# Feed-forward stages: layer-norm sums moved to ScalarE, the residual added by an identity matmul, one scale kept per FP4 block

## The chip, the cores and the metric

The kernel runs on one core of one Trainium2 chip. The metric is the device time of one execution in microseconds (us); less is better. Before the change it is 868.86 us, the median of three runs (866.7 to 873.04). A difference of about 1% is what a measurement of this kernel can tell from none.

## What is computed

The input x is 8 x 512 tokens of 128 features, all float32. Six stages follow one another, each adding to x what it computes from a layer norm of x:

```python
x = x + 0.5 * _L0_ffn_ref(_layernorm(x), router_w, w1_all, w2_all)     # mixture of 8 experts   (moe_a)
x = x + _L0_attn_ref(_layernorm(x), qkv_w, proj_w, alpha_log, beta_log) # linear attention       (linatt)
x = x + 0.5 * _L0_ffn_ref(_layernorm(x), ...)                           #                        (moe_b)
x = x + 0.5 * _L1_ffn_ref(_layernorm(x), w_gate, w_up, w_down)          # FP4 feed-forward       (ffn_a)
x = x + _L1_attn_ref(_layernorm(x), ...)                                # softmax over the batch (att)
x = x + 0.5 * _L1_ffn_ref(_layernorm(x), w_gate, w_up, w_down)          #                        (ffn_b)
```

The change touches the two FP4 feed-forward stages:

```python
def fp4_quant_dequant(x):                       # blocks of 16 along the last axis
    scale = jnp.maximum(jnp.max(jnp.abs(xb), axis=-1, keepdims=True) / 6.0, 1e-12)
    idx = jnp.searchsorted(_MID, jnp.abs(xb / scale))
    return _GRID[idx] * jnp.sign(xb / scale) * scale
def fp4_linear(x, w):
    return jnp.einsum('bsk,nk->bsn', fp4_quant_dequant(x), fp4_quant_dequant(w))
h = jax.nn.silu(fp4_linear(x, w_gate)) * fp4_linear(x, w_up)    # 128 -> 352 features
return fp4_linear(h, w_down)                                    # 352 -> 128
```

## The kernel before

x stays in SBUF from the first stage to the last (`x_sb`, 32 tiles of 128 tokens x 128 features). Each engine runs its own program, written by hand in order, and semaphores join them; no scheduler moves anything. A feed-forward stage takes x in 8 groups (`GROUPS`) of 4 tiles (`TPB`), 512 tokens a group. Its engines run a body of one group each, and the bodies of different engines work on different groups at the same time:

- **VectorE (DVE), `ffn` at L1052**: body(i) first takes the layer-norm statistics of group i+2 (`ln_stats`: four BN_STATS at L754, four BN_AGGR at L761), then multiplies silu(gate) by up for group i (L1085), quantises that product to FP4 (h4), and between h4's divide and its snap adds the down product of group i-1 to x (`residual`, L1059) and starts the quantisation of the normalised x of group i+2 (x4). The class `Fp4` has the steps: `largest` (L700), `scales` (two small instructions, L706 and L708: a negated scale for the end and a nudged one for the reciprocal), `inverse` (L713), `divide` (L717), `snap` (L723), `unbias` (L728), `rescale` (L734). `snap` waits for a magnitude that ScalarE makes of the divided values (L406).
- **ScalarE (ACT), `ffn` at L611**: body(i) normalises group i+2 (`normal`, L435, four tiles), makes the magnitude of group i's h (L406, 1408 elements a row), applies silu and copies up for group i+1 (L625, L627), with the magnitude of x of group i+2 among them, copies the transposed x of group i+2 out of PSUM (`evac_xnT`, L442) and the four transposed tiles of hq of group i (`hidden_T`, L631).
- **TensorE (PE), `ffn` at L1456**: body(i) runs the gate and up products of group i+1, the transposes of x of group i+2 (L1483), the transposes of the quantised h of group i (L1470), and its down products (`down`, three matmuls a tile into PSUM bank 7, L1171 as all products).
- **GpSimd (POOL), `ln_group`**: from mean and variance the two columns with which ScalarE normalises.
- **SyncE** writes each group of the result to DRAM when the residual of the last stage is in (`x_done`).

The order inside ScalarE's body matters here:

```python
if ahead:
    act.wait_ge(s["tr_done"], i + 2)
    normal(i + 2)
act.wait_ge(s["h_divided"], i + 1)
magnitude(fq_h[0], fq_h[1]).then_inc(s["h_sized"], 1)
```

Between four `hidden_T` of group i-1 and the magnitude of group i there is only `normal`. All engines' queues are strictly in order, so whatever is put there is in front of the magnitude.

Of the kernel before, what the change touches and what calls it, by code (L numbers as in the profile page):

```python
# [38 lines left out]
ATT_EPS = 1e-6  # L39
MAGIC = 1.5 * 2.0 ** 22  # L40
TIE = 2.0 ** 100

# [32 lines left out]
def macaron(nc, x, qkv_w, proj_w, alpha_log, beta_log, router_w, w1, w2,  # L75
            in_w, in_b, out_w, out_b, w_gate, w_up, w_down, out):
    with ExitStack() as ctx:
# [36 lines left out]
        negmean = sb("negmean", [P, 8])  # L114
        shift = sb("shift", [P, 8])
        xn = sb("xn", [P, 8, C])
        xnT = sb("xnT", [P, 8 * P])
# [60 lines left out]
        def bank(k, *dims):  # L178
# [7 lines left out]
            if len(dims) == 3:  # L186
# [10 lines left out]

        s_passed_dve, s_passed_pe, s_passed_pool = sem("s_passed_dve"), sem("s_passed_pe"), sem("s_passed_pool")
        PHASES = ["moe_a", "linatt", "moe_b", "ffn_a", "att", "ffn_b"]
        NAMES = ["dve_chain", "pool_chain", "var_ready", "rstd_ready", "xn_ready",  # L200
# [11 lines left out]
                    "h_divided", "h_sized", "x_divided", "x_sized", "hq_ready",  # L212
                    "htr_done", "hT_ready", "down_done"],
        }
# [7 lines left out]
        def group_b(i):  # L222
            return x_sb[:, ds(i * TPB, TPB), :]
# [57 lines left out]
        def _(pool):  # L281
# [22 lines left out]


            ln_group(S["moe_a"], 0, TPB)

# [38 lines left out]
            for ph in PHASES:  # L346
# [18 lines left out]
                elif ph == "att":  # L365
# [13 lines left out]
                    add_bias(TPB - 2)  # L379
                    add_bias(TPB - 1)  # L380
                else:
                    with pool.Fori(1 if ph in ("moe_a", "moe_b") else 0, GROUPS) as i:
                        ln_group(s, i, TPB)
# [3 lines left out]
        def _(act):  # L387
# [31 lines left out]
            def fp4_weights_out():  # L419

                act.wait_ge(s_prep_pe, 4)
                nc.scalar.activation(gateT[:, :], bank(3, FK), ACT.Copy).then_inc(s_prep_act, 1)
                act.wait_ge(s_prep_pe, 5)
                nc.scalar.activation(upT[:, :], bank(4, FK), ACT.Copy).then_inc(s_prep_act, 1)
                act.wait_ge(s_prep_pe, 6)
                nc.scalar.activation(downT[:, :, :], bank(5, 3, P), ACT.Copy).then_inc(s_prep_act, 1)
# [184 lines left out]
            def ffn(s, first):  # L611
# [44 lines left out]
                x_magnitude(0)  # L656
                evac_xnT(s, 0)
# [3 lines left out]
                evac_xnT(s, 1)  # L661
                with act.Fori(0, GROUPS - 2) as i:
                    body(i, True, False)
                body(GROUPS - 2, False, False)
                body(GROUPS - 1, False, True)

            moe(S["moe_a"], S["linatt"], True)
# [9 lines left out]
        def _(dve):  # L677
# [5 lines left out]
            class Fp4:  # L683
# [19 lines left out]
                def scales(self):  # L703
# [3 lines left out]

                    self.t = self.ch.add(nc.vector.tensor_scalar(self.rs, self.mx, (1.0 + 2.0 ** -22) / 6.0, 1e-12,  # L708
                                                                 ALU.mult, ALU.max))

                def inverse(self):
                    self.ch.need(self.t)
                    self.t = self.ch.add(nc.vector.reciprocal(self.rs, self.rs))  # L713

# [337 lines left out]
            def ffn(s, first):  # L1052
                ch = Chain(dve, s["dve_chain"])
                hflat = hid[:, :, :].rearrange("p j f -> p (j f)")

                def residual(i):

                    dve.wait_ge(s["down_done"], i * TPB + TPB)
                    nc.vector.scalar_tensor_tensor(group_b(i), bank(7, TPB, C), 0.5, group_b(i),  # L1059
                                                   ALU.mult, ALU.add).then_inc(s["x_done"], 1)  # L1060

                def x_stream(i):
# [5 lines left out]
                def x_alone(i):  # L1068
                    dve.wait_ge(s["xn_ready"], i + 1)
                    x4 = x_stream(i)  # L1070
                    x4.largest()
                    x4.scales()
                    x4.inverse()
                    x4.divide()
# [3 lines left out]

                def body(i, ahead, behind):

                    if ahead:
                        ln_stats(s, ch, i + 2, TPB, tile_b)

# [7 lines left out]
                    h4.largest()  # L1091
                    h4.scales()
                    h4.inverse()
                    h4.divide()
                    if behind:
                        residual(i - 1)
                    if ahead:
                        dve.wait_ge(s["xn_ready"], i + 3)
                        x4 = x_stream(i + 2)
                        x4.largest()  # L1100
                        x4.scales()
                        x4.inverse()
                        x4.divide()
# [14 lines left out]
                pre = ch.k  # L1118
                ch.start(pre)
                body(0, True, False)  # L1120
                pre += ch.k
                with dve.Fori(1, GROUPS - 2) as i:
                    ch.start((i - 1) * PER["ffn"] + pre)
                    body(i, True, True)
                    assert ch.k == PER["ffn"], ("ffn", ch.k)
                pre += (GROUPS - 3) * PER["ffn"]
                ch.start(pre)
                body(GROUPS - 2, False, True)
                body(GROUPS - 1, False, True)
# [4 lines left out]
                residual(GROUPS - 1)  # L1134
                dve.wait_ge(s["x_done"], GROUPS)
# [10 lines left out]
        def _(pe):  # L1146
# [309 lines left out]
            def ffn(s, first):  # L1456
# [11 lines left out]
                def hidden_transposes(i, j):  # L1468
                    for k in range(3):
                        t = nc.tensor.transpose(bank(5 + j % 2, 3, P)[:, k, :], hq[:, j, P * k:P * k + P], ident[:, :])  # L1470
                    t.then_inc(s["htr_done"], 1)

                def down(i, j):
                    pe.wait_ge(s["hT_ready"], i * TPB + j + 1)
                    for k in range(3):
                        t = mm(bank(7, TPB, C)[:, j, :], hqT[:, j % 2, k, :], downT[:, k, :], start=k == 0, stop=k == 2)
                    t.then_inc(s["down_done"], 1)
# [23 lines left out]
                x_transposes(1)  # L1501
                with pe.Fori(0, GROUPS - 2) as i:
                    body(i, True, False)
# [12 lines left out]

PER = {"moe": 21, "linatt": 8, "att": 24, "ffn": 20}

# [21 lines left out]
```

## Time and profile before

| | |
|---|---|
| median of three runs | 868.86 us |
| the profiled execution, its own time | 870.8 us |
| its span | 869.0 us (1.8 us lie around it) |
| mean granted TensorE clock | 0.896 of full |
| busy: PE, DVE, ACT, POOL | 703.0, 676.8, 466.8, 164.6 us |
| moe_a / linatt / moe_b | about 0 to 143 / 143 to 282 / 282 to 413 us |
| ffn_a / att / ffn_b | about 413 to 562 / 562 to 712 / 712 to 867 us |

"PE busy" counts matmuls that overlap each other; the granted clock has two levels, 1.0 (2.4 GHz) and 0.5 (1.2 GHz), and what lies between in a table is a mean over a stretch. In the timeline rows below a start-to-start distance is the time that an instruction takes of its engine; the duration beside it is up to 0.1 us longer, since neighbours overlap. A float32 product counts as two matmul records, a transpose as one.

### The profile page before, as it was taken

Reading aid. Unit: us, or ns where it says so; the run is one execution under the profiler, and the core shown is the slowest. Engines: PE = TensorE matmul, PEld = TensorE weight load, DVE = VectorE, ACT = ScalarE, POOL = GpSimd, SP = SyncE. Lnnn points to the kernel's source line nnn. Section 1 sums busy time; section 2 is a strip of 40 time slices with the busy share of each in tenths; the row PEclk is TensorE's granted clock in tenths of the full one; section 3 lists DMA queues with packets and bytes.
Section 4 is the critical chain, followed back from the end, with each engine's and each line's share of the span. In section 5 each row is a group of like instructions: output and inputs, shape, how many; then the busy total and the mean of one; then the engine's idle time right before and its main releaser. Section 6 shows DMA issues by size and latency. Waiting matters only on the chain.

```text
span 869.0 us, 17382 instructions
## 1 busy us (share of the span) xinstructions
PE 703.0 (81%) x6018; PEld 533.8 (61%) x6018; DVE 676.8 (78%) x1671; ACT 466.8 (54%) x893; POOL 164.6 (19%) x323
## 2 busy tenths in 40 slices
PE   3999999798986999999585777468989865857774
PEld 2777776677775677776354665436686663546654
DVE  2888787375656578789799999649899956999995
ACT  3787777656460677777464455264323114644552
POOL 4001021645542100101111210022110001112100
PEclk9999999899999899999768788868999987687888
DMA  7000000000000000000000000000000000000000
GB/s 197 2 0 0 0 1 2 3 3 2 0 3 3 1 1 0 0 1 0 1 0 0 0 0 0 1 0 1 1 0 0 1 0 1 12 12 12 12 24 25
DMA packets 13454, 6.99 MB, mean 8 GB/s; under 512 B 1177, under 2 KB 13409, under 8 KB 13409
## 3 DMA queue, kind: packets, MB, share of 16 engines
q1 hardware_dynamic: 10464, 5.26, 2.3%
q10 hardware_dynamic: 2944, 1.12, 0.5%
q8 instruction: 29, 0.48, 0.2%
q14 instruction: 17, 0.13, 0.0%
HBM read 4.28 MB, written 2.10 MB: 7 GB/s over the span
## 4 chain that ended last, share of the span: by engine, by line
PE 60%; DVE 26%; issue 7%; ACT 3%; DMA 1%; POOL 1%; DVEq 0%; SPq 0%; POOLq 0%; ACTq 0%
PE ps L1171 53%; PE ps L1470 4%; DVE ffn_work L723 3%; DVE shared L998 2%; DVE ffn_work L728 2%; DVE picked L900 2%; PE ps L1483 2%; DVE hq L734 1%; DVE x_sb L819 1%; DVE xn L734 1%; ACT xn L435 1%; DVE ffn_work L717 1%; DVE fq_x_max L700 1%; DMA wraw<-ttn_out_proj_weight_dram 1%; DVE attT L906 1%
## 5 line engine op out<-in xcount | busy, mean ns | idle before, releaser
L1171 PEld LDWEIGHTS ps<-w_sb,sq_h 128*128 128x128 f32 x1024 | 131.9, 192 | 68.8 <-ACT sq_h L457 50.7
L819 DVE SCALAR_TENSOR_TENSOR x_sb<-ps,gates,x_sb 128x128 f32 (+1 forms) x512 | 147.8, 345 | 20.4 <-PE ps L1171 12.3
L294 POOL TENSOR_SCALAR vareps<-meanvar 128x4 f32<-128x4 f32 (+1 forms) x44 | 25.0, 568 | 606.4 <-DVEq L763 606.4
L1171 PE MATMUL ps<-w_sb,sq_h 128*128 128x128 f32 x1024 | 138.0, 278 | 0.9 <-ACT sq_h L457 0.9
L1171 PE MATMUL ps<-xnT,w_sb 128*128 128x512 f32 x256 | 135.4, 613 | 0.0
L453 ACT ACTIVATE relu_h<-ps 128x512 f32<-128x512 f32 x128 | 75.7, 591 | 57.6 <-PE ps L1171 57.3
L435 ACT ACTIVATE xn<-x_sb,shift,rstd 128x128 f32 (+1 forms) x192 | 79.8, 481 | 18.3 <-POOL shift L302 18.2
L457 ACT ACTIVATE sq_h<-relu_h 128x512 f32<-128x512 f32 x128 | 80.6, 630 | 4.0
L1483 PE MATMUL ps<-ident,xn 128*128 128x128 f32 x64 | 16.8, 414 | 70.8 <-DVE xn L734 70.8
L1171 PE MATMUL ps<-ident,shared 128*128 128x128 f32 x512 | 64.6, 290 | 10.3 <-DVE shared L998 10.3
L1171 PE MATMUL ps<-downT,hqT 128*128 128x128 f32 x384 | 71.2, 339 | 0.5 <-ACT hqT L631 0.5
L1171 PEld LDWEIGHTS ps<-ident,shared 128*128 128x128 f32 x512 | 63.0, 205 | 13.6 <-DVE shared L998 12.7
L1171 PEld LDWEIGHTS ps<-downT,hqT 128*128 128x128 f32 x384 | 63.6, 246 | 7.4 <-ACT hqT L631 5.8
L1171 PE MATMUL ps<-gateT,xnT 128*128 128x352 f32 x128 | 55.3, 516 | 12.0 <-ACT ffn_work L625 9.2
L631 ACT ACTIVATE hqT<-ps 128x384 f32<-128x384 f32 x64 | 31.2, 491 | 56.6 <-PE ps L1470 54.0
L442 ACT ACTIVATE xnT<-ps 128x512 f32<-128x512 f32 x40 | 23.9, 597 | 69.5 <-PE ps L1483 64.7
L1483 PEld LDWEIGHTS ps<-ident,xn 128*128 128x128 f32 x64 | 11.0, 207 | 79.4 <-DVE xn L734 71.1
L1470 PE MATMUL ps<-ident,hq 128*128 128x128 f32 x192 | 43.8, 373 | 16.7 <-DVE hq L734 16.7
L342 POOL TENSOR_TENSOR shared<-shared 128x128 f32<-128x128 f32 x112 | 51.0, 455 | 28.5 <-ACT shared L508 20.3
L1171 PE MATMUL ps<-upT,xnT 128*128 128x352 f32 x128 | 53.3, 500 | 0.0
L754 DVE BATCH_NORM_STATS2 stats<-x_sb 128x6 f32 (+1 forms) x192 | 41.2, 279 | 13.3 <-DMA x_sb<-in_L_attn_x_dram 9.9
L406 ACT ACTIVATE ffn_work<-ffn_work 128x512 f32<-128x512 f32 (+2 forms) x33 | 33.1, 1003 | 30.2 <-DVE ffn_work L717 30.2
(147 smaller groups left out, 1270.1 us busy)
## 6 DMA issues: line engine op xcount, KB each, us to landing
x_sb<-in_L_attn_x_dram SPq DMA_DIRECT2D x8, 256.0 KB, 6.4
out_dram<-x_sb SPq DMA_DIRECT2D x8, 256.0 KB, 2.3
w_sb<-in_L_ffn_w_all_dram ACTq DMA_DIRECT2D x2, 512.0 KB, 7.4
wraw<-in_L_attn_qkv_w_dram SPq DMA_DIRECT2D x1, 192.0 KB
wraw<-attn_in_proj_weight_dram SPq DMA_DIRECT2D x1, 192.0 KB
fraw<-in_L_ffn_w_down_dram SPq DMA_DIRECT2D x1, 176.0 KB, 3.5
fraw<-in_L_ffn_w_gate_dram SPq DMA_DIRECT2D x1, 128.0 KB, 4.0
fraw<-in_L_ffn_w_up_dram SPq DMA_DIRECT2D x1, 128.0 KB, 3.1
```

The costliest lines, as they stand in the source:

```text
L342: nc.gpsimd.tensor_tensor(st[:, k, :], st[:, k, :], st[:, k - 1, :], ALU.add).then_inc(s["prefix_ready"], 1)
L406: return nc.scalar.activation(m, v, ACT.Abs, scale=2.0 ** 22)
L435: a = nc.scalar.activation(xn[:, into + j, :], tile(i, j), ACT.Identity, scale=rstd[:, j:j + 1], bias=shift[:, j:j + 1])
L453: nc.scalar.activation(relu_h[:, e % 2, :], bank(2 + e % 2, T), ACT.Relu).then_inc(s["relu_done"], 1)
L457: nc.scalar.activation(sq_h[:, e % 2, :], relu_h[:, e % 2, :], ACT.Square).then_inc(s["sq_ready"], 1)
L631: nc.scalar.activation(hqT[:, j % 2, :, :], bank(5 + j % 2, 3, P), ACT.Copy).then_inc(s["hT_ready"], 1)
L723: self.t = self.ch.add(nc.vector.scalar_tensor_tensor(self.v, self.m, MAGIC, self.v, ALU.max, ALU.add))
L754: ch.add(nc.vector.bn_stats(stats[:, j, :], tile(i, j)))
L819: t = nc.vector.scalar_tensor_tensor(tile_b(i, j), bank(4 + e % 4, TPB, C)[:, j, :], gates[:, j, e:e + 1], tile_b(i, j), ALU.mult, ALU.add)
L1171: return nc.tensor.matmul(o, a, b, start=start, stop=stop, **kw)
L1470: t = nc.tensor.transpose(bank(5 + j % 2, 3, P)[:, k, :], hq[:, j, P * k:P * k + P], ident[:, :])
L1483: t = nc.tensor.transpose(bank(0, TPB, P)[:, j, :], xn[:, start + j, :], ident[:, :])
```

## The change

In both feed-forward stages:

1. The layer-norm statistics of groups 2 to 7 go from VectorE to ScalarE. `ln_sum` (four ACTIVATE Copy with `accum_out`) sums each token's features; GpSimd makes the negated mean; `ln_squares` (four ACTIVATE Square with that bias and `accum_out`) sums the squares; GpSimd makes the rest (`ln_from_sums`). Their full output goes to a tile `spare` that nobody reads.
2. The residual add leaves VectorE. `x_under` on TensorE puts x into PSUM bank 7 by one product with the identity, the down products accumulate on it, and `x_out` on ScalarE copies the sum back to x. The factor 0.5 is now in the down weights.
3. `scales` becomes `nudged_scales`, one small instruction less a quantisation; the sign and the nudge go into the weights.

```diff
@@ ScalarE
+                def x_out(i):
+                    act.wait_ge(s["down_done"], i * TPB + TPB)
+                    act.sem_inc(s_passed_act, 1)
+                    nc.scalar.activation(group_b(i), bank(7, TPB, C), ACT.Copy).then_inc(s["x_done"], 1)
+
+                def ln_sum(i):
+                    for j in range(TPB):
+                        a = nc.scalar.activation(spare[:, j, :], tile_b(i, j), ACT.Copy, accum_out=sums[:, 0, j:j + 1])
+                    a.then_inc(s["sum_ready"], 1)
+
+                def ln_squares(i):
+                    act.wait_ge(s["mean_ready"], i - 1)
+                    act.sem_inc(s_passed_act, 1)
+                    for j in range(TPB):
+                        a = nc.scalar.activation(spare[:, j, :], tile_b(i, j), ACT.Square, bias=negmean[:, j:j + 1],
+                                                 accum_out=sums[:, 1, j:j + 1])
+                    a.then_inc(s["square_ready"], 1)
+
-                def body(i, ahead, last):
+                def body(i, ahead, last, further=False):
                     if ahead:
 
                         act.wait_ge(s["tr_done"], i + 2)
                         normal(i + 2)
+                    if not (type(i) is int and i == 0):
+                        x_out(i - 1)
+                    if further:
+                        ln_sum(i + 3)
                     act.wait_ge(s["h_divided"], i + 1)
                     magnitude(fq_h[0], fq_h[1]).then_inc(s["h_sized"], 1)
...
+                    if further:
+                        ln_squares(i + 3)
                     if ahead:
                         evac_xnT(s, i + 2)
...
                 normal(1)
+                ln_sum(2)
+                ln_squares(2)
                 x_magnitude(0)
@@ VectorE
-                def residual(i):
-
-                    dve.wait_ge(s["down_done"], i * TPB + TPB)
-                    nc.vector.scalar_tensor_tensor(group_b(i), bank(7, TPB, C), 0.5, group_b(i),
-                                                   ALU.mult, ALU.add).then_inc(s["x_done"], 1)
...
-                    if ahead:
-                        ln_stats(s, ch, i + 2, TPB, tile_b)
...
-                    h4.scales()
-                    h4.inverse()
+                    h4.nudged_scales()
+                    h4.inverse(h4.sl)
                     h4.divide()
-                    if behind:
-                        residual(i - 1)
@@ TensorE
+                def x_under(i):
+
+                    if not (type(i) is int and i == 0):
+                        pe.wait_ge(s["x_done"], i)
+                    mm(bank(7, TPB, C), ident[:, :], group_b(i), start=True, stop=False, skip_group_check=True)
...
                         x_transposes(i + 2)
+                    x_under(i)
                     pe.wait_ge(s["hq_ready"], i + 1)
                     hidden_transposes(i, 0)
```

How the programs stand, first ScalarE, in the loop of ffn_a, from the last tile of `normal` to the magnitude. `xn` is the normalised x, `ffn_work` with 1408 columns the magnitude, with 352 columns silu. Before:

```order
L435 ACTIVATE xn<-x_sb,shift,rstd 128x128
L638 REGISTER_ALU
L406 ACTIVATE ffn_work<-ffn_work 128x1408
L624 ISA
L625 ACTIVATE ffn_work<-ps 128x352
```

The same place after the change, where the lines have other numbers (of the four sums the first and the last are shown):

```order
L461 ACTIVATE xn<-x_sb,shift,rstd 128x128
L660 ISA
L662 ISA
L662 ACTIVATE x_sb<-ps 128x512
L666 ISA
L666 ACTIVATE spare,sums<-x_sb 128x128
...
L666 ACTIVATE spare,sums<-x_sb 128x128
L686 REGISTER_ALU
L432 ACTIVATE ffn_work<-ffn_work 128x1408
```

A copy of 512 columns, behind a wait for the down products, and four ACTIVATEs with an accumulator now stand between `normal` and the magnitude.

TensorE, in the same loop, from the transposes of x to the first down products (`ps<-ident,xn` are the transposes of x, `ps<-ident,hq` those of h). Before:

```order
L1480 REGISTER_ALU
L1483 MATMUL ps<-ident,xn 128x128 x4
L1470 MATMUL ps<-ident,hq 128x128 x6
L1474 ISA
L1171 MATMUL ps<-downT,hqT 128x128 x3
```

and after the change:

```order
L1533 REGISTER_ALU
L1536 MATMUL ps<-ident,xn 128x128 x4
L1217 ISA
L1217 MATMUL ps<-x_sb,ident 128x512
L1516 MATMUL ps<-ident,hq 128x128 x6
L1526 REGISTER_ALU
L1217 MATMUL ps<-downT,hqT 128x128 x3
```

One product of 512 columns now stands between the transposes of x, which come last from VectorE, and those of h.

## Rows read from the trace of the kernel before

**Rows 1.** Timeline of DVE: start us, us, operation, in brackets idle before.
```profile
495.43 0.86 DVE L754 BATCH_NORM_STATS2 stats<-x_sb 128x6 f32 x4
...
497.06 1.63 DVE L1085 TENSOR_TENSOR ffn_work<-ffn_work 128x1408 f32<-128x1408 f32 x1 [0.23 <-DVE meanvar L761]
...
500.37 0.21 DVE L706 TENSOR_SCALAR fq_h_s<-fq_h_max 128x88 f32<-128x88 f32 x1
...
503.27 0.69 DVE L1059 SCALAR_TENSOR_TENSOR x_sb<-ps,x_sb 128x512 f32 x1 [0.18 <-PE ps L1171]
503.87 0.68 DVE L700 TENSOR_REDUCE fq_x_max<-xn 128x32 f32<-128x512 f32 x1
...
505.88 1.62 DVE L723 SCALAR_TENSOR_TENSOR ffn_work<-ffn_work 128x1408 f32<-128x1408 f32 x1
...
511.93 0.69 DVE L734 TENSOR_TENSOR xn<-ffn_work,fq_x_s 128x512 f32<-128x512 f32 x1
...
514.17 1.63 DVE L1085 TENSOR_TENSOR ffn_work<-ffn_work 128x1408 f32<-128x1408 f32 x1 [0.24 <-DVE meanvar L761]
...
529.64 1.62 DVE L1085 TENSOR_TENSOR ffn_work<-ffn_work 128x1408 f32<-128x1408 f32 x1
...
542.79 1.62 DVE L1085 TENSOR_TENSOR ffn_work<-ffn_work 128x1408 f32<-128x1408 f32 x1
```

**Rows 2.** Timeline of ACT in the same round of ffn_a.
```profile
502.12 1.65 ACT L435 ACTIVATE xn<-x_sb,shift,rstd 128x128 f32 x4
503.67 1.36 ACT L406 ACTIVATE ffn_work<-ffn_work 128x1408 f32<-128x1408 f32 x1
```

**Rows 3.** Timeline of PE in the same round.
```profile
495.56 1.11 PE L1483 MATMUL ps<-ident,xn 128*128 128x128 f32 x4 [4.61 <-DVE xn L734]
496.47 1.49 PE L1470 MATMUL ps<-ident,hq 128*128 128x128 f32 x6
497.90 1.65 PE L1171 MATMUL ps<-downT,hqT 128*128 128x128 f32 x6
499.34 0.85 PE L1470 MATMUL ps<-ident,hq 128*128 128x128 f32 x3
...
501.10 0.49 PE L1470 MATMUL ps<-ident,hq 128*128 128x128 f32 x3
...
502.94 0.76 PE L1171 MATMUL ps<-gateT,xnT 128*128 128x352 f32 x2
```

**Rows 4.** Busy us (instructions) by stretch: PE, PEld, DVE, ACT, POOL; then PEclk, DMA, GB/s.
```profile
494.00:495.00 1.00, 0.00 (x0) 0.00 (x0) 0.96 (x3) 0.00 (x0) 0.00 (x0) 0.55 0.00 0
500.00:501.00 1.00, 1.00 (x7) 1.00 (x7) 0.93 (x4) 0.49 (x1) 0.40 (x2) 0.54 0.00 0
...
607.00:608.00 1.00, 1.00 (x7) 1.00 (x6) 1.00 (x2) 0.00 (x0) 0.00 (x0) 0.50 0.00 0
```

**Rows 5.** Timeline of PE in att, just ahead of the last stretch of rows 4.
```profile
605.69 9.04 PE L1171 MATMUL ps<-ident,shared 128*128 128x128 f32 x64 [2.27 <-DVE shared L998]
```

**Rows 6.** Timeline of PE in moe_b, a product of 512 columns and its neighbour.
```profile
289.47 1.02 PE L1171 MATMUL ps<-xnT,w_sb 128*128 128x512 f32 x2
290.33 1.05 PE L1171 MATMUL ps<-w_sb,sq_h 128*128 128x128 f32 x8
```

**Rows 7.** Groups by line and shape: xcount | busy us, mean ns of one | idle before.
```profile
L435 ACT ACTIVATE xn<-x_sb,shift,rstd 128x128 f32 x128 | 53.4, 481 | 0.0
...
L417 ACT ACTIVATE wT<-ps 128x128 f32<-128x128 f32 x1 | 0.3, 273 | 0.0
```

**Rows 8.** Timeline of PE, then of ACT, in the last but one group of ffn_a.
```profile
542.92 0.87 PE L1470 MATMUL ps<-ident,hq 128*128 128x128 f32 x6 [0.90 <-DVE hq L734]
...
546.35 0.49 ACT L631 ACTIVATE hqT<-ps 128x384 f32<-128x384 f32 x1 [0.51 <-PE ps L1470]
```

**Rows 9.** Timeline of ACT at the start of ffn_a and of ffn_b: the first magnitude of x.
```profile
416.21 0.63 ACT L406 ACTIVATE ffn_work<-ffn_work 128x512 f32<-128x512 f32 x1 [0.88 <-DVE ffn_work L717]
...
720.12 0.61 ACT L406 ACTIVATE ffn_work<-ffn_work 128x512 f32<-128x512 f32 x1
```

More of the change, by code:

```diff
@@ L40 @@
 MAGIC = 1.5 * 2.0 ** 22
+NUDGE = 2.0 ** -22
 TIE = 2.0 ** 100
@@ L115, in macaron @@
         shift = sb("shift", [P, 8])
+        sums = sb("sums", [P, 2, TPB])
+        spare = sb("spare", [P, TPB, C])
         xn = sb("xn", [P, 8, C])
@@ L301, in ln_group, with ln_from_sums @@
                 pool.wait_ge(s["pool_chain"], 3 * i + 3)
+                nc.gpsimd.tensor_tensor(shift[:, 0:n], negmean[:, 0:n], rstd[:, 0:n],
+                                        ALU.mult).then_inc(s["rstd_ready"], 1)
+            def ln_from_sums(s, i, n):
+                pool.wait_ge(s["sum_ready"], i - 1)
+                pool.sem_inc(s_passed_pool, 1)
+                nc.gpsimd.tensor_scalar(negmean[:, 0:n], sums[:, 0, 0:n], -1.0 / C, None,
+                                        ALU.mult).then_inc(s["mean_ready"], 1)
+                pool.wait_ge(s["square_ready"], i - 1)
+                pool.sem_inc(s_passed_pool, 1)
+                nc.gpsimd.tensor_scalar(vareps[:, 0:n], sums[:, 1, 0:n], 1.0 / C, LN_EPS, ALU.mult,
+                                        ALU.add).then_inc(s["moment_chain"], 1)
+                pool.wait_ge(s["moment_chain"], 2 * (i - 2) + 1)
+                nc.gpsimd.tensor_tensor(rstd[:, 0:n], vareps[:, 0:n], minus_half[:, 0:n],
+                                        ALU.pow).then_inc(s["moment_chain"], 1)
+                pool.wait_ge(s["moment_chain"], 2 * (i - 2) + 2)
                 nc.gpsimd.tensor_tensor(shift[:, 0:n], negmean[:, 0:n], rstd[:, 0:n],
@@ L380, in _ @@
                     add_bias(TPB - 1)
+                elif ph in ("ffn_a", "ffn_b"):
+                    ln_group(s, 0, TPB)
+                    ln_group(s, 1, TPB)
+                    with pool.Fori(2, GROUPS) as i:
+                        ln_from_sums(s, i, TPB)
                 else:
-                    with pool.Fori(1 if ph in ("moe_a", "moe_b") else 0, GROUPS) as i:
+                    with pool.Fori(1, GROUPS) as i:
                         ln_group(s, i, TPB)
@@ L661, in ffn @@
                 evac_xnT(s, 1)
-                with act.Fori(0, GROUPS - 2) as i:
-                    body(i, True, False)
+                body(0, True, False, True)
+                with act.Fori(1, GROUPS - 3) as i:
+                    body(i, True, False, True)
+                body(GROUPS - 3, True, False)
                 body(GROUPS - 2, False, False)
                 body(GROUPS - 1, False, True)
+                x_out(GROUPS - 1)
             moe(S["moe_a"], S["linatt"], True)
@@ L1071, in x_alone @@
                     x4.largest()
-                    x4.scales()
-                    x4.inverse()
+                    x4.nudged_scales()
+                    x4.inverse(x4.sl)
                     x4.divide()
@@ L1077, in x_alone, with body @@
                     x4.rescale()
-                def body(i, ahead, behind):
-                    if ahead:
-                        ln_stats(s, ch, i + 2, TPB, tile_b)
+                def body(i, ahead, further):
                     dve.wait_ge(s["up_ready"], i * TPB + TPB)
@@ L1118, in ffn @@
                 pre = ch.k
[L1119 to L1123, printed above, removed]
+                with dve.Fori(0, GROUPS - 3) as i:
+                    ch.start(i * PER["ffn"] + pre)
                     body(i, True, True)
                     assert ch.k == PER["ffn"], ("ffn", ch.k)
[L1126 to L1129, printed above, removed]
+                ch.start((GROUPS - 3) * PER["ffn"] + pre)
+                body(GROUPS - 3, True, False)
+                body(GROUPS - 2, False, False)
+                body(GROUPS - 1, False, False)
                 if first:
@@ L1475, in down @@
                     for k in range(3):
-                        t = mm(bank(7, TPB, C)[:, j, :], hqT[:, j % 2, k, :], downT[:, k, :], start=k == 0, stop=k == 2)
+                        t = mm(bank(7, TPB, C)[:, j, :], hqT[:, j % 2, k, :], downT[:, k, :], start=False, stop=k == 2,
+                               skip_group_check=True)
                     t.then_inc(s["down_done"], 1)
@@ L1501, in ffn @@
                 x_transposes(1)
-                with pe.Fori(0, GROUPS - 2) as i:
+                body(0, True, False)
+                with pe.Fori(1, GROUPS - 2) as i:
                     body(i, True, False)
@@ L1513, in _ @@
             ffn(S["ffn_b"], False)
-PER = {"moe": 21, "linatt": 8, "att": 24, "ffn": 20}
+PER = {"moe": 21, "linatt": 8, "att": 24, "ffn": 10}
 _INS = ['L0_attn_x', 'L0_attn_qkv_w', 'L0_attn_proj_w', 'L0_attn_alpha_log', 'L0_attn_beta_log',
```

24 lines of the change are left out of this document (14 added, 10 removed).

## The prediction

> **What bounds the kernel now.** I read the whole-span table first, then the chain that ended last, then, since the change touches only ffn_a and ffn_b, the timelines of DVE, ACT and PE over one round of ffn_a. A round runs from one L1085 of VectorE to the next: 497.06 to 514.17, 17.11 us, and four rounds of a stage are alike [rows 1]. In it VectorE has hardly an idle moment: 0.23 us ahead of L1085 and 0.18 ahead of L1059 [rows 1]. PE stands idle for 4.61 us and waits for VectorE's last instruction, the rescaled x [rows 3]. So VectorE's own work sets the round.
>
> There is a second limit close behind, a ring through three engines. I count it from the start of the transposes of x on PE, at 495.56 [rows 3]:
> - transposes of x and h and the down products interleaved with their copies: ACT has made its last hqT copy at 502.12, so 6.56 us [rows 2, 3];
> - `normal` of the next group, to 503.67: 1.55 [rows 2];
> - the magnitude of h, 1.36: done at 505.03 [rows 2];
> - VectorE from the snap of h (505.88) to the end of x's rescale (511.93 + 0.69 = 512.62): 6.74 [rows 1]; hand-overs, 0.07 together.
>
> That is 16.28 us. The magnitude was ready 0.85 us before VectorE took it up; the ring has 0.83 us to spare in a round of 17.11. It has no more than that, and all the work that the change adds to ACT and PE must be looked for in it.
>
> The clock belongs to this ring. It falls to half (1.2 GHz) while PE waits (0.55 on the mean in the microsecond from 494) and is full again only at about 500.9 (0.54 in the microsecond from 500) [rows 4]; so the transposes and the first down products of every round run at half clock.
>
> **The change part by part.**
>
> VectorE loses the statistics, 495.43 to 497.06, 1.63 us; L1059 with its idle, 0.18 + (503.87 - 503.27) = 0.78; and one small scale in each of two quantisations (the longer 0.21 us, and overlapped with its neighbours, so I take 0.2 for both) [rows 1]. Its own work falls from 17.11 to 14.5 us a round. If VectorE stayed the bound, this would be the round.
>
> But the ring grows by three terms, all of which stand in its order as the programs show:
>
> *x_under on PE*, between the transposes of x and those of h. One product of 512 columns takes 0.86 us at full clock, from 289.47 to 290.33 [rows 6]. At half clock it is twice that, 1.72, as six transposes take 1.43 (496.47 to 497.90) there [rows 3]. I lay it into the round of rows 3: transposes of h start at 2.63 instead of 0.91 after the start, first down product at 4.06, end at 5.50. By then the clock is up (it rose 5.4 us after the start [rows 4]), and the second down product, 1.12 us at mostly half clock before (start at 499.34 + 0.64, to 501.10), takes 0.76 and the transposes beside it 0.33 instead of 0.64. The last hqT copy ends about 1.05 us later than before, at 7.61. If the clock rises no earlier, all 1.72 count.
>
> *x_out on ACT*: 512 columns out of PSUM, 0.5 us after `normal` (a copy of 384 columns takes 0.49 [rows 8]). Its wait for the down products costs nothing, since they end under `normal` (502.94, before 503.67 [rows 2, 3]).
>
> *ln_sum on ACT*: no row shows an ACTIVATE with an accumulator. Below, a plain one of 128 columns takes 273 ns, 0.18 us apart when it overlaps its neighbour as the others do; above, the one with two pointer operands takes 481 ns, 0.39 apart (1.55 for four) [rows 2, 7]. The accumulator's result has to be written too, which might cost still more than a pointer; I set twice the upper row, 0.8, as the far end. For the sum, without pointers, I take the middle of the two rows, 0.29, four are 1.16; for the squares, with one pointer, 0.39, four are 1.56. The Trainium skill, "ScalarE: Activation LUTs", section "What ACT_TABLE_LOAD costs", gives 186 ns + 0.833 ns a column, 93 ns more for each pointer operand and 93 ns overlap between neighbours. The trace agrees for L435 (479 by the page, 481 measured). By it, an accumulator being free, the four sums would be 0.8 us instead of 1.16 and each round 0.36 shorter; it gives no price of the accumulator.
>
> The ring is then 7.61 + 1.55 + 0.50 + 1.16 + 1.36 + 6.74 + 0.07 = 19.0 us, against VectorE's 14.5. VectorE waits about 4.5 us a round, at the snap of h, for the magnitude. The bound moves from VectorE to the ring, and the round gets longer: 19.0 against 17.11.
>
> *ln_squares* stand behind the silus and cost nothing in the rounds: the magnitude ends at 12.2 after the start of the ring, silus and the magnitude of x take about 3.7, the squares 1.56, together 17.4 of 19.0. They have 1.6 us of cover; at 0.8 us apiece they would take it all.
>
> Now one stage, from the first L1085 on.
> - First body: only VectorE's saving counts, since its magnitude isn't late: -1.85.
> - Four full rounds, 514.17 being the end of the last: 4 x (19.0 - 17.11) = +7.6.
> - The body from 514.17 to 529.64, 15.47 [rows 1]: `normal` and x_out, no ln_sum: 19.0 - 1.16 = 17.8: +2.4.
> - The body to 542.79, 13.15 [rows 1]: x_out after the down products (8.5), 0.5, magnitude 1.36, then snap to the end of h, 4.86 as before: 15.3: +2.1.
> - Last body: nothing; the copy by ACT takes the place of L1059's 0.69.
> Together +10.2 for each of the two stages.
>
> *The start of each stage.* ln_sum(2), the mean on GpSimd and ln_squares(2) stand in front of the first magnitude of x, for which VectorE waits. In ffn_a ACT was idle for 0.88 us ahead of it [rows 9]; 1.16 + 0.4 (mean and hand-overs) + 1.56 = 3.1 less 0.88: +2.2. In ffn_b it had no idle [rows 9]: +3.1.
>
> Sum, with the clock at half at the start of each round: 2 x 10.2 + 5.3 = +25.7.
>
> **The clock.** In warm rounds the ring is shorter. The last but one group shows it: from the transposes of h at 542.92 to the last copy's end at 546.84, 3.92 [rows 8]. With 0.45 and 0.86 in front: 5.23 instead of 7.61, so a ring of 16.6. PE's idle before x's transposes would be about 3.8 us instead of 4.61 (gate and up products j = 2, 3 wait for silu, which comes after the magnitude). Is that enough for the clock to fall? In att it fell after only 2.27 us of idle [rows 4, 5]. So most rounds will be cold; I take one in four to be warm, three of 12 over both stages, 3 x 2.4 = -7.2. That leaves +18.5 on the profiled execution's 870.8. The median of the runs, 868.86, is 0.2% below it; on that basis I forecast 887.
>
> **The rivals.**
> - *The clock stays up* (chance 0.20). Rounds of 16.6: per stage -1.85 - 4 x 0.5 - 0.2 for the two shorter bodies = -4.1; with the starts -8.2 + 5.3 = -2.9: 866 us, no difference that can be measured. For it: PE is busy at either side of a shorter idle. Against it: the fall after 2.27 us.
> - *The change does what it says* (0.10): VectorE remains the bound at 14.5, because ACT reaches the magnitude in time. Per stage -1.85 - 4 x 2.6 - 1.0 (15.47 to 14.5) = -13.3, with the starts -26.6 + 5.3 = -21: 848 us. This is the side of faster. It decides at a ring of under 17.1: it would need a copy done and sums finished before the down products' end, that is ACT's magnitude no later than 505.9 in the row's time; against it stands the strict order of ACT's program. A weaker form, warm rounds with sums 0.18 apart, gives 16.2 a round and about 860.
> - *The accumulator is dear* (0.08): at 0.8 apiece the sums cost 2.0 us more in each of eight full rounds and each start 3.7 more: +24 on 887, 911. At 0.5 apiece, 0.84 a round and 1.3 a start: +9, 896.
> - The forecast, cold rounds for the most part: 0.62, own range 876 to 897.
>
> **The numbers.** Slower by over 1% (above 877.5) holds nearly all of the forecast and the dear accumulator, 0.69; within 1% the rest of it and the warm rival, 0.21; faster 0.10. The range goes from a little under the warm rival, 864, to a little over the forecast with the accumulator at 0.5, 899.
>
> **What would show it.** VectorE idle for 2 us or more ahead of the snap of h in each full round, released by ACT's magnitude (right), or none (the second rival). Rounds between L1085s of 19.0 cold and 16.6 warm. On ACT `normal`, x_out, four sums and the magnitude without a gap; the sums' spacing, 0.29 or not. x_under at 1.7 us and a PEclk of 0.5 from before x's transposes. The first snap of x in ffn_b 3.1 us later after `normal`. Wrong would be: PE out of the chain that ended last in the two stages, or PEclk at 1.0 through them.

## The result, and the profile after

| | before | after |
|---|---|---|
| median of the runs | 869.64 us (866.7 to 873.04) | 886.79 us (886.09 to 889.69) |
| the profiled execution, its span | 870.8, 869.0 us | 889.69, 888.0 us |
| busy: PE, DVE, ACT | 703.0, 676.8, 466.8 us | 708.9, 649.5, 505.7 us |

The change makes the kernel slower: 1.0206 times the time of before, 95% interval 1.0168 to 1.0244. In the two profiled executions VectorE is busy 27 us less and the kernel takes 19 us longer: taking work off VectorE brought no time.

In the waits of DVE in the kernel after (us in total, times, longest), two lines lead into the feed-forward:

```profile
DVE fq_x_max L755 <- ACT xn L461: 29.6, 10, 3.7
DVE ffn_work L784 <- ACT ffn_work L432: 27.8, 16, 5.6
```

The first is the first step of x's quantisation, which waits for `normal`; the second is the snap of h, which waits for the magnitude. DVE's timeline of one cold round of ffn_a (cold: PE's clock is at half through its first part), to hold against [rows 1] (L1137 is L1085 of before, L784 is L723):

```profile
503.93 1.62 DVE L1137 TENSOR_TENSOR ffn_work<-ffn_work 128x1408 f32<-128x1408 f32 x1
...
508.21 1.62 DVE L778 TENSOR_TENSOR ffn_work<-ffn_work,fq_h_r 128x1408 f32<-128x1408 f32 x1
513.57 0.69 DVE L755 TENSOR_REDUCE fq_x_max<-xn 128x32 f32<-128x512 f32 x1 [3.73 <-ACT xn L461]
...
516.48 1.62 DVE L784 SCALAR_TENSOR_TENSOR ffn_work<-ffn_work 128x1408 f32<-128x1408 f32 x1 [0.90 <-ACT ffn_work L432]
...
523.15 1.62 DVE L1137 TENSOR_TENSOR ffn_work<-ffn_work 128x1408 f32<-128x1408 f32 x1
```

19.22 us from L1137 to L1137, where it was 17.11 [rows 1]; 3.73 + 0.90 = 4.63 of them idle. ACT in this round, to hold against [rows 2] (L657 copies hqT, L461 is `normal`, L662 x_out, L666 the sums, L432 the magnitude):

```profile
511.33 0.49 ACT L657 ACTIVATE hqT<-ps 128x384 f32<-128x384 f32 x1 [0.51 <-PE ps L1516]
511.89 1.65 ACT L461 ACTIVATE xn<-x_sb,shift,rstd 128x128 f32 x4
513.44 0.57 ACT L662 ACTIVATE x_sb<-ps 128x512 f32 x1
513.92 0.30 ACT L666 ACTIVATE spare<-x_sb 128x128 f32 x1
514.12 0.19 ACT L666 ACTIVATION_READ_ACCUMULATOR spare<-x_sb 128x1 f32 x1
514.21 0.30 ACT L666 ACTIVATE spare<-x_sb 128x128 f32 x1
...
515.09 1.36 ACT L432 ACTIVATE ffn_work<-ffn_work 128x1408 f32<-128x1408 f32 x1
```

and PE, against [rows 3] (the second line is x_under):

```profile
504.07 1.11 PE L1536 MATMUL ps<-ident,xn 128*128 128x128 f32 x4 [3.80 <-DVE xn L795]
504.97 1.92 PE L1217 MATMUL ps<-x_sb,ident 128*128 x2
506.68 1.49 PE L1516 MATMUL ps<-ident,hq 128*128 128x128 f32 x6
508.11 1.65 PE L1217 MATMUL ps<-downT,hqT 128*128 128x128 f32 x6
```

The ring can be read off step by step: transposes of x at 504.07 to the last hqT copy's end at 511.82, 7.75; `normal` 1.55 and 0.07 of hand-over; x_out 0.48; four sums 1.17; the magnitude 1.36; snap (516.48) to the end of x's rescale, 6.75; with the small hand-overs 19.2.

Not all rounds are alike. The L1137s of ffn_a are 14.42, 18.05, 19.07, 18.13, 19.22, 16.83 and 14.53 us apart, those of ffn_b within 0.13 of these. The second to the fifth are the full rounds, those with `ln_sum`. Each has a stretch at half clock. In the two longer ones it ended 5.7 and 6.0 us after the start of x's transposes, in the two shorter ones 3.2 and 3.7 us after it. In three of the four it began ahead of the transposes; in the fourth, whose transposes began at 485.94, the clock fell 0.23 us behind their start, and they took less than the 1.11 us of the cold round:

```profile
485.94 0.94 PE L1536 MATMUL ps<-ident,xn 128*128 128x128 f32 x4 [3.81 <-DVE xn L795]
```

Two stretches of the granted clock (the column behind POOL) show the difference, for this short round and for the long one above:

```profile
489.00:490.00 1.00, 0.99 (x6) 0.66 (x5) 0.93 (x3) 0.67 (x2) 0.00 (x0) 0.71 0.00 0
...
509.00:510.00 1.00, 1.00 (x7) 1.00 (x7) 0.84 (x1) 0.00 (x0) 0.00 (x0) 0.50 0.00 0
```

Where the 19.0 us of span are, from the same events in both traces: start of ffn_a (from `normal(1)` to the first L1085 or L1137) +2.7, its bodies +6.7, start of ffn_b +3.5, its bodies +6.5. That is 19.4; the stages that the change does not touch differ by +2.7 (before ffn_a) and -3.0 (att), which I take for the difference between two executions: over the 14 traces of this document, which share their code there, the start of `normal(1)` in ffn_a lies between 412.93 and 416.77, and the time from the last write of x in ffn_a to the start of `normal(1)` in ffn_b between 152.8 and 156.3 us.

The added time does not come from a colder clock. From the first to the eighth L1085 or L1137 of ffn_a the mean granted clock is 0.79 before and 0.87 after, and in ffn_b the same: PE is at half clock for less time than before, and the rounds are longer all the same.

### The profile page after: what moved, and what is told of

It is laid out like the page before. It is cut to its first block, busy times and chain, and to the rows that moved or that the text cites. A ratio compares the mean times of both kernels' runs of the same rounds, so it can differ in the third digit from the quotient of the medians.

```text
span 888.0 us, 17404 instructions
## 1 busy us (share of the span) xinstructions
PE 708.9 (80%) x6050; PEld 526.4 (59%) x6050; DVE 649.5 (73%) x1527; ACT 505.7 (57%) x1101; POOL 165.8 (19%) x323
## 4 chain that ended last, share of the span: by engine, by line
PE 58%; DVE 23%; ACT 8%; issue 7%; POOL 1%; DMA 1%; ACTq 1%; SPq 0%; DVEq 0%; POOLq 0%
PE ps L1217 51%; DVE ffn_work L784 3%; PE ps L1516 3%; DVE ffn_work L789 2%; DVE shared L1059 2%; ACT xn L461 2%; ACT ffn_work L432 2%; DVE picked L961 2%; PE ps L1536 2%; ACT spare L666 1%; DVE hq L795 1%; DVE xn L795 1%; DVE x_sb L880 1%; DVE attT L967 1%; DMA wraw<-ttn_out_proj_weight_dram 1%
## 5 line engine op out<-in xcount | busy, mean ns | idle before, releaser
L298 POOL TENSOR_SCALAR vareps<-meanvar 128x4 f32<-128x4 f32 (+1 forms) x32 | 7.7, 240 | 442.6 <-DVEq L824 442.6
L461 ACT ACTIVATE xn<-x_sb,shift,rstd 128x128 f32 (+1 forms) x192 | 79.7, 480 | 17.0 <-POOL shift L306 16.5
L1536 PE MATMUL ps<-ident,xn 128*128 128x128 f32 x64 | 15.0, 379 | 70.3 <-DVE xn L795 70.3
L1217 PEld LDWEIGHTS ps<-ident,shared 128*128 128x128 f32 x512 | 61.2, 200 | 15.2 <-DVE shared L1059 14.7
L657 ACT ACTIVATE hqT<-ps 128x384 f32<-128x384 f32 x64 | 30.9, 490 | 65.6 <-PE ps L1516 64.1
L1217 PE MATMUL ps<-downT,hqT 128*128 128x128 f32 x384 | 60.8, 303 | 1.1 <-ACT hqT L657 1.0
L784 DVE SCALAR_TENSOR_TENSOR ffn_work<-ffn_work 128x512 f32<-128x512 f32 (+2 forms) x33 | 38.3, 1161 | 27.8 <-ACT ffn_work L432 27.8
L1217 PEld LDWEIGHTS ps<-downT,hqT 128*128 128x128 f32 x384 | 53.1, 210 | 7.7 <-ACT hqT L657 6.1
L1217 PEld LDWEIGHTS ps<-gateT,xnT 128*128 128x128 f32 x128 | 24.5, 211 | 43.6 <-ACT ffn_work L651 30.7
L1516 PEld LDWEIGHTS ps<-ident,hq 128*128 128x128 f32 x192 | 31.8, 184 | 30.1 <-DVE hq L795 16.4
```

The lines of the kernel that those rows point to most:

```text
L461: a = nc.scalar.activation(xn[:, into + j, :], tile(i, j), ACT.Identity, scale=rstd[:, j:j + 1], bias=shift[:, j:j + 1])
L657: nc.scalar.activation(hqT[:, j % 2, :, :], bank(5 + j % 2, 3, P), ACT.Copy).then_inc(s["hT_ready"], 1)
L784: self.t = self.ch.add(nc.vector.scalar_tensor_tensor(self.v, self.m, MAGIC, self.v, ALU.max, ALU.add))
L1217: return nc.tensor.matmul(o, a, b, start=start, stop=stop, **kw)
L1536: t = nc.tensor.transpose(bank(0, TPB, P)[:, j, :], xn[:, start + j, :], ident[:, :])
```

## The experiments

All are the kernel after the change ("after") with the edit shown, unless it says otherwise. What a run gained is its median against the 886.79 us of after; ratios are to the kernel before, whose median on these chips was 869.96 to 870.96 us, up to 1.3 us above the 869.64 of the result, so a gain may be larger by up to that. Round times are the distances of L1137 (or the line that answers to it) in ffn_a, without the last body.

**sums_later.** The four sums leave the ring.

```diff
-                    if further:
-                        ln_sum(i + 3)
                     act.wait_ge(s["h_divided"], i + 1)
...
                     if further:
+                        ln_sum(i + 3)
                         ln_squares(i + 3)
```

> Based on the changed kernel (886.8 us); the four sums of the group ahead stand behind the silus instead of between normal and the magnitude of h. Theory (a ring through PE, ACT and VectorE sets the round, and these 1.16 us are a term of it): each of 8 full rounds gets shorter by about 1.16 us, from 18.6 to 17.5, and the time falls to about 877.5. Rival (ScalarE is simply loaded, it doesn't matter where the sums stand): no change, 885 to 888.

878.46 us, 1.0079 (1.0053 to 1.0106): 8.3 us gained. Rounds 14.42, 17.07, 17.26, 17.32, 17.18, 16.94, 14.72. The snap of h no longer waits; what is left is the wait for `normal`, 2.56 to 2.81 us in these rounds. At the same clock a round therefore gains about 0.90, the wait at the snap, and not the 1.16 of the sums: the branch by x's quantisation is then the longer. A round of ffn_b shows it, whose half-clock stretch ends 5.95 us after the start of the ring: 18.25 us, where the one of 19.22 in after had 6.00. The other rounds are shorter because the clock rises sooner, too.

**under_early.** x_under before the wait for x, in PE's idle time.

```diff
+                    x_under(i)
                     if ahead:
                         x_transposes(i + 2)
-                    x_under(i)
```

> Based on the changed kernel (886.8 us); PE runs the product of x with the identity ahead of the transposes of x, in the time in which it waited for VectorE, instead of behind them. Theory (ring): 1.7 us at half clock come off the ring in each of 12 bodies, if nothing else moves by 1.2 to 1.7 each: 867 to 873. Rival (the product only takes the place of idle time that the ring had anyway, or the clock gets colder, since the wait is split): 880 to 887.

872.84 us, 1.0015 (0.9998 to 1.0033): 14.0 us gained. Rounds 14.42, 15.80, 17.30, 17.18, 17.12, 15.94, 14.16. It is the dearest of the parts: in the cold round of above x_under took 1.71 us. A part of the gain may be the clock's: x's transposes now begin at full clock in all 12 bodies, where in after they began at half in six of the 12. How the gain divides between the two, no run shows.

**out_later.** `x_out(i - 1)` goes from in front of the magnitude to right behind it (the call moved with its condition).

> Based on the changed kernel (886.8 us); ScalarE copies x out of PSUM behind the magnitude of h instead of ahead of it. Theory (ring): 0.5 us less in each of 10 bodies and 1.4 in the two in which that copy waited for the last down product: 8 us less, 879. Rival (the copy is hidden behind the down products): no change.

879.97 us, 1.0115 (1.0083 to 1.0147): 6.8 us gained.

**start_later.** At a stage's start `x_magnitude(0)` goes in front of `ln_sum(2)` and `ln_squares(2)` (one line moved).

> Based on the changed kernel (886.8 us); at the start of both stages the sums and squares of group 2 stand behind the first magnitude of x, where ScalarE has 3.4 us of idle time, instead of ahead of it. Theory (the starts cost 2.7 and 3.45 us, all of it exposed): 6 us less, about 881. Rival (the start is hidden behind PE's slow first products): no change.

881.54 us, 1.0141 (1.0094 to 1.0188): 5.3 us gained, as the prediction priced the two starts together.

**filled.** Three products of 512 columns that nobody reads, where PE stands idle.

```diff
+                x_filler = w1_sb[:, 0:TPB, :].rearrange("p e f -> p (e f)")
...
                     if ahead:
+                        for _ in range(3):
+                            mm(bank(0, T), ident[:, :], x_filler)
                         x_transposes(i + 2)
```

> Based on the changed kernel (886.8 us); three more float32 products of 512 columns (identity by weights, into a PSUM bank that is free then, results unused) stand in PE's idle time ahead of the transposes of x. They add work and compute nothing that is used. Theory (the clock at half lengthens the ring): the clock stays up, a full round takes 16.6 us instead of 18.6, and the time falls to about 868 in spite of 31 us more work on PE. Rival (the clock has no part in it, the ring's length is the same at either level): 887 or, if the filler delays the transposes, above.

867.26 us, 0.9966 (0.9949 to 0.9984). More work on PE made the kernel 19.5 us faster than after. Rounds 14.42, 16.51, 16.69, 16.70, 16.69, 15.51, 13.22. PE's timeline of a round, of which the first line is the three products:

```profile
491.01 2.74 PE L1217 MATMUL ps<-w_sb,ident 128*128 128x512 f32 x6
494.98 0.66 PE L1538 MATMUL ps<-ident,xn 128*128 128x128 f32 x4 [1.23 <-DVE xn L795]
495.47 1.02 PE L1217 MATMUL ps<-x_sb,ident 128*128 x2
```

and the same stretch of 20 us of the table by stretch, with PEclk third from the end, first of after, then of filled:

```profile
504.00:524.00 20.00, 14.46 (x63) 10.49 (x64) 15.06 (x17) 12.08 (x36) 3.95 (x6) 0.84 0.00 0
```
```profile
504.00:524.00 20.00, 16.97 (x75) 10.95 (x76) 17.79 (x18) 14.98 (x38) 3.01 (x4) 1.00 0.00 0
```

The transposes of x take 0.66 instead of 1.11 us and the identity product 0.86 (494.98 + 0.49 to the next start) instead of 1.71, at a clock of 1.00. The last hqT copy ends 5.21 us after the start of the ring. The round of 16.6 that the prediction worked out for full clock is there, 16.7.

**residual_only and sums_only.** One part of the change alone; both keep the dropped scale. residual_only leaves the statistics on VectorE (`ln_stats` in the body, no `ln_sum`, no `ln_squares`); sums_only leaves the residual there (no `x_under`, no `x_out`, `residual` with 0.5 between h4's divide and x's quantisation, and no 0.5 in the down weights).

> Only the residual by the identity product and the dropped scale, the layer-norm statistics on VectorE as before the change. Theory (ring): the ring loses the 1.16 us of the sums against the changed kernel, and the starts cost nothing; a full round takes about 17.5 us; about 877, that is slower than before the change (869.6) by about 7. Rival (the sums are what costs, the residual by itself is a gain of VectorE's 0.78 us a round): under 869.6, about 860.

871.97 us, 1.0019 (0.9996 to 1.0042), 5 us less than expected. Rounds 16.17, 18.00, 17.66, 16.93, 16.72, 15.26, 15.23: the longest is about what the prediction's terms give at half clock without the sums (19.0 - 1.16 = 17.8), the others show less time at half clock, and I had not allowed for that.

> Only the layer-norm sums on ScalarE and the dropped scale, the residual on VectorE as before the change. Theory (ring): the ring is 16.3 + 1.16 = 17.4 us, 0.3 more than VectorE's round of before; with the first body 1.85 shorter and the starts 6 us longer the time is about 874. Rival (VectorE's work sets the round, 15.3 us now): 869.6 - 8 x 1.8 - 3.7 + 6, about 858.

872.18 us, 1.0018 (0.9997 to 1.004). It was expected at 874. Against before on the same chip each part alone is 2.0 and 2.2 us slower, and both intervals include no change; both together cost 17.2. The traces show why neither gains: in a full round VectorE is idle for 1.0 to 2.3 us in residual_only, mostly ahead of x's quantisation, and for 1.1 to 2.7 in sums_only, mostly ahead of the residual, where it waits for the down products. What a part takes off VectorE comes back as a wait. That the two together cost so much more than apart fits a ring that was level with VectorE before the change (below), onto which both now come; no run of its own shows it.

**spread.** `normal` of group i+3 in two halves among the hqT copies of body i, where ACT waits for PE anyway.

```diff
-                def body(i, ahead, last, further=False):
-                    if ahead:
-
-                        act.wait_ge(s["tr_done"], i + 2)
-                        normal(i + 2)
...
+                def body(i, ahead, last, further=False, then=False):
...
                     if ahead:
                         evac_xnT(s, i + 2)
-                    for j in range(TPB):
-                        hidden_T(i, j)
+                    if then:
+                        normal_part(i + 3, 0, 2)
+                    hidden_T(i, 0)
+                    hidden_T(i, 1)
+                    if then:
+                        normal_part(i + 3, 2, 4)
+                    hidden_T(i, 2)
+                    hidden_T(i, 3)
...
-                body(0, True, False, True)
+                normal(2)
+                body(0, True, False, True, True)
```

> Based on the changed kernel (886.8 us); normal of the next group is taken out of its place ahead of the magnitude and put in two halves in front of and between the four hqT copies, where ScalarE waits for PE. Theory (ring): 1.55 us come off the ring, of which the first half may delay the first copy a little: 1.0 to 1.5 in each of 10 bodies, 872 to 877. Rival (VectorE's wait is for x only, or the halves delay PE's down products by as much): 884 or more.

883.25 us, 1.0153 (1.0102 to 1.0204): the first theory missed. ACT's timeline says where the 1.55 us went:

```profile
488.87 0.49 ACT L657 ACTIVATE hqT<-ps 128x384 f32<-128x384 f32 x1 [0.51 <-PE ps L1529]
490.56 0.60 ACT L662 ACTIVATE x_sb<-ps 128x512 f32 x1 [1.20 <-PE ps L1230]
```

x_out waits 1.20 us for the last down product, and 1.11 to 1.21 in each of the 12 bodies. With `normal` in front of it this wait was covered, as the prediction had said; with `normal` gone it takes its place.

**spread_out_later.** spread with x_out behind the magnitude, to test just that.

> The run spread, with x_out moved behind the magnitude as well. Theory (in spread the wait of x_out for the last down product, 1.20 us of idle, took the place of normal): without x_out in front of it, the magnitude goes behind the sums, which wait for nothing. Its ring loses 1.2 of wait and 0.5 of copy against spread: full rounds of about 16 to 16.7 instead of 17.9 (mean of spread), 866 to 871 us. Rival (the lost gain lay elsewhere, for instance in hqT copies that are later because half of normal stands between them): only the 0.5 of the copy comes off, rounds 17.4, 878 or more.

861.73 us, 0.9851 (0.9806 to 0.9897), 21.5 us less than spread; better than I expected of it. Rounds 14.41, 16.13, 15.85, 15.08, 15.84, 14.41, 12.91. The same move brought 6.8 us in after; the 14.7 more that it brings here are what 12 waits of 1.2 us come to. The wait for the down product was the cause. The four executions lie between 856.32 and 869.83.

**all_moved.** sums_later, under_early, out_later and start_later in one kernel.

> All four moves that paid one by one: sums behind the silus, x_under ahead of the transposes of x, x_out behind the magnitude, and the sums and squares of group 2 at the start behind the magnitude of x(0). Theory (the ring through three engines is what bounds): it is as long as before the change, 16.3 at most and about 15.5 where the clock rises early, against VectorE's 14.5. Full rounds of 15.5 to 16.3 by 17.2 before, 853 to 861 us. First rival (the savings overlap, since the moved work meets another wait, such as squares that now come late for the silus or the copy that frees bank 7): 862 or more. Second rival (VectorE becomes the bound): rounds of 14.5, 848.

853.85 us, 0.9821 (0.9786 to 0.9856): with spread_out_later one of the two versions that are clearly ahead of both kernels, and the faster by its median. It is 32.9 us faster than after; the four moves one by one gained 8.3 + 14.0 + 6.8 + 5.3 = 34.4. With each run taken against before on its own chip it is 34.1 against 38.6, so they overlap by little. But the rounds, 14.42, 15.08, 16.51, 16.64, 17.29, 14.81, 12.23, go up to 1 us over the 16.3 that I gave the ring at half clock. DVE's timeline of the longest:

```profile
499.92 0.69 DVE L754 TENSOR_REDUCE fq_x_max<-xn 128x32 f32<-128x512 f32 x1 [2.79 <-ACT xn L461]
...
501.85 1.62 DVE L783 SCALAR_TENSOR_TENSOR ffn_work<-ffn_work 128x1408 f32<-128x1408 f32 x1
```

The snap of h waits for nothing. What stands between `normal` and the snap is not the magnitude (1.36) but x's own quantisation up to its divide, 1.93 (499.92 to 501.85). The ring has two branches here, one by the magnitude and one by x's quantisation, and this one is now the longer: 6.81 to the last copy's end, 0.07, `normal` until its last tile can be used 1.68, 1.93, and 6.80 from the snap to x's rescale, 17.29.

**all_spread and all_spread_filled.** all_moved with the halves of `normal` as in spread; the second also with the three products of filled.

> As all_moved, with normal of group i+3 in two halves among the hqT copies of body i, so that it isn't between the last copy and the magnitude. Theory: the ring loses up to 1.55 more and is 14.7 at most if the halves fit in ACT's idle time between the copies (0.5 to 1.8 us each); VectorE at 14.5 bounds: full rounds 14.5 to 15.0, 842 to 849 us. Rival (PE's waits grow as the copies come later, for the halves of 0.8 us stand in their way, and the clock stays low): rounds of 15.5 or more, no better than all_moved.

> As all_spread, with three products of 512 columns that nobody reads ahead of the transposes of x in each round, where PE would be idle. If VectorE already bounds in all_spread, they change nothing (within 2 us of it, 842 to 849). If the ring at half clock still bounds there, they take it away and this one is 3 us or more faster. Rival: the products are too long at half clock (1.7 us each) and stand in front of the transposes of x: rounds longer than in all_spread.

873.95 us, 1.0041 (1.0024 to 1.0059), and 868.75 us, 0.9983 (0.9962 to 1.0004). They were expected at 842 to 849, so they missed by 25 and 20 us. The full rounds of all_spread in ffn_a are 20.49, 17.88, 17.56 and 17.32 us, as its rival had it (15.5 or more). ACT, then PE, in all_spread:

```profile
502.93 0.57 ACT L468 ACTIVATE xnT<-ps 128x512 f32<-128x512 f32 x1
504.92 0.88 ACT L682 ACTIVATE xn<-x_sb,shift,rstd 128x128 f32 x2 [1.42 <-POOL shift L324]
505.70 0.84 ACT L657 ACTIVATE hqT<-ps 128x384 f32<-128x384 f32 x2
```
```profile
501.71 0.82 PE L1528 MATMUL ps<-ident,hq 128*128 128x128 f32 x6
506.23 1.65 PE L1229 MATMUL ps<-downT,hqT 128*128 128x128 f32 x6 [3.69 <-ACT hqT L657]
```

The two moves don't agree. sums_later makes the squares late (they wait 0.88 us for the negated mean), so GpSimd's `shift` comes late, and spread has put the instruction that needs it in front of the hqT copies. ACT waits 1.42 us for GpSimd with two finished transposes behind it in its queue, PE stands idle for 3.69 us in the middle of the ring, and its down products start at half clock. This cause is read from the trace; no run takes that wait away and leaves the rest. spread_out_later supports it: there the sums stand in front of the magnitude, ACT waits for `shift` at most 0.38 us, but for the first body of each stage (1.02 and 1.30), and the kernel is 12.2 us faster than all_spread. In all_spread_filled the wait of 1.42 us is still there, and its products stand in the way, as its rival said: x's transposes start about 1.0 us behind VectorE's multiply instead of 0.14. It is 5.2 us faster than all_spread nevertheless; in the traces most of that lies in the first full round of each stage (15.30 for 20.49, and 15.25 for 17.57).

Not tried: sums left in front of the magnitude with `normal` spread and x_under early, which by spread_out_later and under_early might lie below all_moved.

## Why the prediction was right, and where it was not

- **The bound moves from VectorE to the ring: right.** All of VectorE's 4.6 us of idle time in a round hang on ACT; forecast were 4.5. Every move that shortened the ring, as the traces show it, made the kernel faster.
- **VectorE's own work, 14.5: right**; the first bodies, where nothing is late, are 14.42 in both stages.
- **x_under at 1.72 cold: right** (504.97 to 506.68, 1.71). The last copy ended 7.75 after the start of the ring, forecast 7.61: the second down product ran at half clock longer than I had laid it.
- **x_out 0.5, its wait covered: right** (0.48), and spread shows how narrow that cover was.
- **The sums at 0.29: right to 0.01** (0.29 apart), squares 0.385. That is luck: the middle of two rows was a choice, and the trace shows another composition: a plain ACTIVATE that takes 0.20 and a separate read of the accumulator that takes 0.09. Of the Trainium skill, "ScalarE: Activation LUTs", section "What ACT_TABLE_LOAD costs", I said that with a free accumulator the four sums would be 0.8 us; the trace has that share for the ACTIVATEs alone, 4 x 0.20, and 0.37 more for the reads.
- **The place of the wait: half wrong.** I put all 4.5 us at the snap, for the magnitude. 3.73 of them are one step earlier, where VectorE wants the normalised x. The sign that the prediction named, 2 us or more of idle ahead of the snap, did not appear; there it was 0.90. The sum stayed right since the longer branch still ended at the magnitude: from the end of `normal`, x_out, sums and magnitude are 3.0 us, x's quantisation 2.1 with its hand-over, and the difference is the 0.90 at the snap.
- **"The ring has 0.83 us to spare": wrong as a step.** I counted only the branch by the magnitude, 16.28. By the other, in the rows of before: 6.56 to the last copy, `normal` until L700 could start 1.68 (taken from after, 511.89 to 513.57, since in before L700 waits for nothing), L700 to the snap 2.01 (503.87 to 505.88), then 6.74 and 0.05: 17.04 of 17.11. Ring and VectorE were level in a cold round. It did not change this sum, but it made my second rival (848, rounds of 14.5) look nearer than it was, and my bound for all_moved 1 us too low.
- **Squares hidden: right** in the rounds; they stopped being so in all_moved and all_spread, where the sums stand right in front of them.
- **Body sums.** Four full rounds +5.4 and +5.3 us a stage against the +7.6 worked out at half clock: 18.6 a round on the mean, not 19.0, against 17.26 before on the mean, not 17.11. The sixth body +1.4 (forecast +2.4), the seventh +1.4 (+2.1). The starts +2.7 and +3.5 (+2.2 and +3.1). The first bodies -1.8 as forecast.
- **The clock: right in size, wrong in form.** I took one round in four to be warm, 7.2 us. None was warm throughout: each had a stretch at half clock, and a full round was shorter by up to 1.2 us where that stretch was short. The sign "a PEclk of 0.5 from before x's transposes" held in six of the eight full rounds. That a clock which fell after 2.27 us of idle must fall after 3.8 was too simple: it was full at the end of 3.81 us of idle in the other two. Against the 25.7 us for all-cold rounds the same events give 19.4: 4.5 us less in the full rounds, 3.4 less in the sixth and seventh bodies, 0.9 more at the starts and 0.6 more in the last bodies. That the forecast of 887 was met by 0.2 us is luck: the allowance of 7.2 us was right in sum and not where I put it.
- **The rival of the clock that stays up** (866) is what filled does (867.26): its price was right, its condition was not met by the change itself.

## What to carry to other kernels

Before work is moved off the busiest engine, follow the data once round through all the engines, by every branch, and see how much shorter than the round the longest way is; here it was 0.07 us, and what was moved landed on it. The work may go to the same engine and yet cost nothing, if it stands behind the instruction that the others wait for: the same change with four pieces in other places is 1.8% faster than before instead of 2.1% slower. And a move that pays by itself can undo another: the first instruction of a queue that waits holds all that is behind it, so with each new order ask what each wait was covered by.

## What the runs showed of the hardware

- An ACTIVATE with an accumulator leaves two rows: itself, and an ACTIVATION_READ_ACCUMULATOR of 0.19 us that takes 0.09 of the engine. Four of 128 columns take 1.17 us, with a pointer operand 1.54.
- In after PE's idle time ahead of x's transposes was 2.6 or 2.7 us in the first full round of a stage and 3.8 in the other three. The clock was at half at its end in six of these eight rounds, the first ones among them; in the two others it was full and fell 0.23 and 0.14 us later. With 1.23 us (filled) it stayed up. In one stage of all_moved it went both ways with the same 3.12 us of idle: here four transposes took 1.11 us, there 0.66. I did not settle what decides between them.

```profile
491.36 1.11 PE L1535 MATMUL ps<-ident,xn 128*128 128x128 f32 x4 [3.12 <-DVE xn L794]
...
508.65 0.66 PE L1535 MATMUL ps<-ident,xn 128*128 128x128 f32 x4 [3.12 <-DVE xn L794]
```
